# Cross-attention slot sums split between TensorE and VectorE in a decoder layer, with the tick offsets around it moved

## The reference

```python
x = x + attn(layernorm(x))                       # causal, 16 heads of 16
x = x + xattn(ctx, ctx, layernorm(x), ssm, D, 8)  # long convolution of key-value products
x = x + ffn(layernorm(x))                        # 4-bit weights, 256 -> 2048 (gate, up) -> 256
```

```python
kv = einsum('bhil,bhjl->bijhl', k, v)
out = causal_conv(kv, ssm_kernel) + kv * D
out = einsum('bijhl,bhil->bjhl', out, q)
```

## Time and profile before

| | |
|---|---|
| median of 3 runs | 279.81 us |
| the profiled execution | 280.03 us |
| its span, first to last instruction | 278.3 us |
| busy: TensorE (PE) | 250.9 us, 90% |
| busy: VectorE (DVE) | 162.5 us, 58% |
| busy: GpSimd (POOL) | 149.3 us, 54% |
| busy: ScalarE (ACT) | 129.9 us, 47% |
| mean granted TensorE clock | 0.972 of full speed |

### The profile page before, as it was taken

How to read it: one execution, slowest core, us unless ns; L and a number is a source line. 1 busy time by engine, 2 the same in 40 slices (tenths; PEclk the granted TensorE clock), 3 DMA queues, 4 the chain that set the end, 5 groups by cost and what they waited for, 6 DMA issues and landing times.

```text
span 278.3 us, 5004 instructions
## 1 busy us (share of the span) xinstructions
PE 250.9 (90%) x1872; PEld 161.9 (58%) x1872; DVE 162.5 (58%) x280; ACT 129.9 (47%) x281; POOL 149.3 (54%) x172
## 2 busy tenths in 40 slices
PE   7999999965999887895598998999999999999993
PEld 7765775533665655673454655556665566556662
DVE  2888523989786999668658364251725446131114
ACT  2454665545466666764555254331435243432230
POOL 3278464413116596759988995228354554723330
PEclk9999999999799999978979999999999999999998
DMA  6998969130300000000420030000303000000004
GB/s 200 389 318 199 181 224 173 30 114 4 117 1 4 2 1 6 1 2 0 124 102 2 0 115 0 1 4 0 113 2 113 3 2 0 0 2 0 0 2 151
DMA packets 15104, 18.81 MB, mean 68 GB/s; under 512 B 1448, under 2 KB 12776, under 8 KB 15080
## 3 DMA queue, kind: packets, MB, share of 16 engines
q1 hardware_dynamic: 13832, 16.13, 21.4%
q10 hardware_dynamic: 1248, 2.36, 2.7%
HBM read 15.21 MB, written 3.15 MB: 66 GB/s over the span
## 4 chain that ended last, share of the span: by engine, by line
PE 56%; DVE 5%; POOL 4%; issue 3%; ACT 2%; DVEq 0%; POOLq 0%; ACTq 0%
PE bank L980 30%; PE bank L1150 15%; PE bank L1165 2%; PE bank L1163 2%; POOL w L492 1%; PE bank L1177 1%; DVE o_sb L851 1%; POOL arena L476 1%; PE bank L1179 1%; PE bank L1108 1%; DVE XN L946 1%; ACT XN L651 1%; POOL rstd L403 1%; POOL arena L479 1%; PE bank L1203 1%
## 5 line engine op out<-in xcount | busy, mean ns | idle before, releaser
L500 POOL TENSOR_TENSOR QK<-QK 128x512 f16<-128x512 f32 x31 | 35.9, 1160 | 56.0 <-ACT QK L625 56.0
L894 DVE SCALAR_TENSOR_TENSOR QK<-bank,QK 128x512 f32<-128x512 f32 x32 | 22.0, 689 | 61.2 <-PE bank L980 61.2
L635 ACT ACTIVATE QK<-bank 128x512 f32<-128x512 f32 x32 | 19.1, 597 | 70.5 <-PE bank L980 70.3
L980 PE MATMUL bank<-xTh,Wa 128*128 128x512 f16 x128 | 41.9, 389 | 0.0
L980 PE MATMUL bank<-xTh,Wb 128*128 128x512 f16 x128 | 40.7, 379 | 0.0
L476 POOL TENSOR_TENSOR arena<-Ys,qx 128x640 f32<-128x640 f32 x16 | 25.1, 1568 | 2.0 <-ACT qx L665 2.0
L980 PE MATMUL bank<-xTl,Wa 128*128 128x512 f16 x64 | 25.0, 391 | 0.0
L980 PE MATMUL bank<-xTl,Wb 128*128 128x512 f16 x64 | 24.3, 379 | 0.0
L816 DVE TENSOR_REDUCE mx<-bank 128x8 f32<-128x1024 f32 x16 | 19.4, 1212 | 7.7 <-PE bank L1073 7.6
L1150 PE MATMUL bank<-Wa,QK 128*128 128x256 f16 x192 | 23.6, 273 | 0.0
L403 POOL TENSOR_TENSOR rstd<-veps,nhalf 128x1 f32<-128x1 f32 x16 | 9.6, 597 | 25.6 <-ACT veps L643 25.6
(11 more groups left out here) (145 smaller groups left out, 509.8 us busy)
## 6 DMA issues: line engine op xcount, KB each, us to landing
arena<-in_ker SPq DMA_DIRECT2D x2, 1024.0 KB, 12.0
QK<-qk_scratch SPq DMA_DIRECT2D x8, 256.0 KB, 5.9
arena<-in_ctx SPq DMA_DIRECT2D x2, 768.0 KB, 7.8
qk_scratch<-Wa SPq DMA_DIRECT2D x12, 128.0 KB, 3.4
arena<-in_codes SPq DMA_DIRECT2D x4, 384.0 KB
QK<-qk_scratch SPq DMA_DIRECT2D x8, 128.0 KB, 5.8
arena<-in_gu_scale SPq DMA_DIRECT2D x4, 256.0 KB
out<-XN SPq DMA_DIRECT2D x4, 256.0 KB, 2.4
```

The lines of the kernel that those rows point to most:

```text
L500: g_.tensor_tensor(il[:, u % IR], val[:, u % VR], ih[:, u % IR], ALU.subtract).then_inc(s_il, 1)
L635: s_.activation(val[:, u % VR], bank[2 * (u % 2)][:, :], ACT.Gelu_apprx_tanh, scale=1.0 / W_GAIN).then_inc(s_gel, 1)
L894: v_.scalar_tensor_tensor(out=val[:, u % VR], in0=bank[2 * (u % 2) + 1][:, :], scalar=UP_SCALE, in1=val[:, u % VR], op0=ALU.mult, op1=ALU. ...
L980: ins = mmul(out, a(c), w(c), start=(n == 0), stop=(n == 3 * len(chunks) - 1))
```

## The change

- The half 1 of the slot sums leaves VectorE. In `T_RT` TensorE adds it from Z directly: eight float32 matmuls, one for each slot, whose stationary operand is every eighth word of Z's second half. R keeps half 0 and becomes half as large. The step waits for the reduce only after the residual's matmul, and then for the second half of Z.
- `T_MIX2` goes from 12 to 11, `T_SPLIT` from 1 to 2, `T_PROJ` from 9 to 8 (and behind `T_ATT` in its tick, which leaves its place in the cyclic order as it was). `CONV_RATE` goes from 2 to 1. Units 6 and 7 and the decoding of groups 2 and 3 come one tick earlier. TICKS stays 30.
- The order of steps within a tick is another on every engine. On TensorE the query's transposes (`T_QT`) go ahead of the scores, and `T_YT` ahead of the transposed scores.

```diff
-        R = sb("R", [P, 2, 2 * H, HD])
+        R = sb("R", [P, 2, H, HD])
...
-         T_QT, T_MIX, T_MIX2, T_SUM, T_SUM2, T_RT, T_LN3, T_RSTD3, T_APPLY3, T_YT) = (
-            0, 1, 3, 4, 5, 6, 7, 7, 8, 9, 8, 9, 9, 10, 11, 12, 12, 12, 13, 13, 14, 15, 15)
+         T_QT, T_MIX, T_MIX2, T_SUM, T_RT, T_LN3, T_RSTD3, T_APPLY3, T_YT) = (
+            0, 2, 3, 4, 5, 6, 7, 7, 8, 8, 8, 9, 9, 10, 11, 11, 12, 13, 13, 14, 15, 15)
-        CONV_RATE = 2
+        CONV_RATE = 1
-        UNIT_TICKS = (22, 23, 24, 24, 25, 26, 28, 29)
+        UNIT_TICKS = (22, 23, 24, 24, 25, 26, 27, 28)
-        DECODE = (1, 5, 19, 23)
+        DECODE = (1, 5, 18, 22)
...
                 if lc == 0:
                     pool.wait_ge(s_qx, 2 * b + 2)
                     if b >= 2:
-                        pool.wait_ge(s_r, 2 * (b - 1))
+                        pool.wait_ge(s_r, b - 1)
+                elif b >= 2:
+                    pool.wait_ge(s_rt, b - 1)
...
-            def sum_slots(b, half):
+            def sum_slots(b):
-                ve.wait_ge(s_z, 4 * b + 2 * half + 2)
+                ve.wait_ge(s_z, 4 * b + 2)
-                v_.tensor_reduce(R[:, b % 2, H * half:H * half + H],
-                                 view(Z[:, b % 2], [[NSLOT, H * HD], [1, NSLOT]], 1024 * half),
+                v_.tensor_reduce(R[:, b % 2], view(Z[:, b % 2], [[NSLOT, H * HD], [1, NSLOT]]),
                                  AX.X, ALU.add).then_inc(s_r, 1)
...
                     take(6, s_x2, b + 1)
-                    pe.wait_ge(s_r, 2 * b + 2)
                     pe.wait_ge(s_x1, b + 1)
                     mmul(bank[6][:, 0:D], ident[:, :], X[:, b, :], start=True, stop=False, skip_group_check=True)
-                    for c in range(2):
-                        last = mmul(bank[6][:, P * c:P * c + P],
-                                    R[:, b % 2, H * c:H * c + H, :].rearrange("p h i -> p (h i)"),
-                                    ident[:, :], start=False, stop=(c == 1), skip_group_check=True)
+                    pe.wait_ge(s_r, b + 1)
+                    mmul(bank[6][:, 0:P], R[:, b % 2].rearrange("p h i -> p (h i)"),
+                         ident[:, :], start=False, stop=True, skip_group_check=True)
+                    pe.wait_ge(s_z, 4 * b + 4)
+                    for slot in range(NSLOT):
+                        last = mmul(bank[6][:, P:2 * P], view(Z[:, b % 2], [[NSLOT, P]], 1024 + slot),
+                                    ident[:, :], start=False, stop=(slot == NSLOT - 1), skip_group_check=True)
                     last.then_inc(s_rt, 1)
```

More of the change, by code:

```diff
@@ L504, in _ @@
             for t in range(TICKS):
-                for b in batch(t, T_MIX2):
-                    conv_products(b, 1)
+                for j in early_decode(t, 2):
+                    decode_scale(j, 1)
+                for b in batch(t, T_MIX):
+                    conv_products(b, 0)
                 for b in batch(t, T_RSTD3):
@@ L509, in _ @@
                     rstds(2, b, 1)
-                for j in early_decode(t, 2):
-                    decode_scale(j, 1)
+                for b in batch(t, T_RSTD2):
+                    pool.wait_ge(s_veps[1], b + 1)
+                    rstds(1, b, 1)
+                for b in batch(t, T_MIX2):
+                    conv_products(b, 1)
+                for j in early_decode(t, 1):
+                    decode_scale(j, 0)
                 for h in conv_heads(t + 1):
@@ L514, in _ @@
                         products(h)
[L515 to L521, removed]
                 for u in early_units(t):
@@ L657, in _ @@
             for t in range(TICKS):
+                for b in batch(t, T_LN3):
+                    sc.wait_ge(s_rt, b + 1)
+                    s_.activation(X[:, b, :], bank[6][:, 0:D], ACT.Copy).then_inc(s_x2, 1)
+                for b in batch(t, T_RSTD3):
+                    ln_eps(2, b)
+                for b in batch(t, T_APPLY3):
+                    ln_apply(2, b)
+                for b in batch(t, T_MPT):
+                    sc.wait_ge(s_mpt, b + 1)
+                    if b >= 2:
+                        sc.wait_ge(s_rows[b % 2], 32 * (b // 2))
+                    s_.activation(mT[:, b % 2, :], bank[7][0:2 * H, 0:P],
+                                  ACT.Copy).then_inc(s_mt, 1)
+                    exp_max(b)
+                for h in conv_heads(t):
+                    conv_out(h, 0)
+                    conv_out(h, 1)
+                for b in batch(t, T_OT):
+                    sc.wait_ge(s_ot, b + 1)
+                    if b >= 2:
+                        sc.wait_ge(s_proj, b - 1)
+                    s_.activation(oT[:, b % 2], bank[7][:, 0:D].rearrange("p (c t) -> p c t", c=2),
+                                  ACT.Copy).then_inc(s_ott, 1)
                 for b in batch(t, T_QT):
@@ L667, in _ @@
                                   ACT.Copy).then_inc(s_qx, 1)
[L668 to L687, removed]
                 for b, p in pair_of_groups(t, T_ST):
@@ L691, in _ @@
                     pv_out(b)
+                for b in batch(t, T_LN2):
+                    sc.wait_ge(s_proj, b + 1)
+                    s_.activation(X[:, b, :], bank[7][:, 0:D], ACT.Copy).then_inc(s_x1, 1)
                 for b in batch(t, T_RSTD2):
                     ln_eps(1, b)
+                for b in batch(t, T_APPLY2):
+                    ln_apply(1, b)
                 for u in early_units(t):
                     unit(u)
+                for j in early_decode(t, 2):
+                    w_hi_step(j)
+                    if j + 1 < EARLY:
+                        load_codes(sc, j + 1)
                 for b in batch(t, T_YT):
@@ L700, in _ @@
                                   ACT.Copy).then_inc(s_yth, 1)
[L701 to L712, removed]
             for u in range(2 * EARLY, UNITS):
@@ L879, in w_lo @@
                                         op0=ALU.mult, op1=ALU.subtract).then_inc(s_ffl, 1)
-            def sum_slots(b, half):
-                ve.wait_ge(s_z, 4 * b + 2 * half + 2)
-                if half == 0 and b >= 2:
+            def sum_slots(b):
+                ve.wait_ge(s_z, 4 * b + 2)
+                if b >= 2:
                     ve.wait_ge(s_rt, b - 1)
-                v_.tensor_reduce(R[:, b % 2, H * half:H * half + H],
-                                 view(Z[:, b % 2], [[NSLOT, H * HD], [1, NSLOT]], 1024 * half),
+                v_.tensor_reduce(R[:, b % 2], view(Z[:, b % 2], [[NSLOT, H * HD], [1, NSLOT]]),
                                  AX.X, ALU.add).then_inc(s_r, 1)
@@ L897, in _ @@
             for t in range(TICKS):
[L898 to L905, removed]
                 for h in conv_heads(t + 1):
@@ L908, in _ @@
                         products(h)
+                for b in batch(t, T_SUM):
+                    sum_slots(b)
+                for b, p in pair_of_groups(t, T_SCORES):
+                    pair_max(b, p)
+                for j in early_decode(t, 3):
+                    w_lo(j)
+                for b in batch(t, T_LN3):
+                    ve.wait_ge(s_x2, b + 1)
+                    ln_stats(2, b)
+                for b in batch(t, T_SPLIT):
+                    max_pieces(b)
                 for b in batch(t, T_LN2):
@@ L915, in _ @@
                     codes_join(j)
[L916 to L920, removed]
                 for b in batch(t, T_NORM):
@@ L1157, in _ @@
             for t in range(TICKS):
[L1158 to L1163, removed]
+                for b in batch(t, T_QT):
+                    take(6, s_qx, 2 * b + 2)
+                    pe.wait_ge(s_xn[1], b + 1)
                     for c in range(2):
-                        last = mmul(bank[7][:, 0:D], oT[:, b % 2, c, :], wo[:, c, :], start=False, stop=(c == 1))
-                    last.then_inc(s_proj, 1)
+                        last = t_.transpose(bank[6][:, P * c:P * c + P], XN[:, b, P * c:P * c + P], ident[:, :])
+                    last.then_inc(s_qt, 1)
                 for b, p in pair_of_groups(t, T_SCORES):
@@ L1186, in _ @@
                     mmul(bank[7][0:2 * H, 0:P], mp[:, b % 2, :], identh[:, :], start=True, stop=True).then_inc(s_mpt, 1)
[L1187 to L1197, removed]
+                for h in conv_heads(t):
+                    convolve(h, 0)
+                    convolve(h, 1)
                 for b in batch(t, T_YT):
@@ L1204, in _ @@
                     last.then_inc(s_yt, 1)
+                for b, p in pair_of_groups(t, T_ST):
+                    if p == 0:
+                        pe.wait_ge(s_rows[b % 2], 32 * (b // 2 + 1))
+                    scores_t(b, p)
                 for b in batch(t, T_TOK):
@@ L1223, in _ @@
                     attend(b, g)
+                for b in batch(t, T_PROJ):
+                    take(7, s_x1, b + 1)
+                    pe.wait_ge(s_ott, b + 1)
+                    if b == 0:
+                        pe.wait_ge(s_w[3], 16)
+                    mmul(bank[7][:, 0:D], ident[:, :], X[:, b, :], start=True, stop=False)
```

(6 more changed lines are left out.)

## The result

The changed kernel takes 317.64 us (median of 4 runs, 313.87 to 320.99) against 280.26 us: a ratio of 1.1305, 95% interval 1.1239 to 1.137. It is 37 us slower, and the forecast was 286.9. The sign was right; the size lies far outside the range of 277 to 296.

What follows compares the result with a forecast made beforehand. PE's order was taken to bound most periods, GpSimd one. Convolutions -4.3, QT +1.7, periods +5.3 and late ticks +4.4 sum to +7.1 us on 280.03, 287.1, or 286.9 us as median; range 277 to 296.

Steps and rivals of the forecast that it cites:

- What bounds it: From the first RT, PE's order from T_OT to the suffix sum plus some 3 us of normalising, not the busy DVE.
- the four periods that PE sets: Periods from 91.15 to 129.33 us: RT's added passes count whole, less 0.6 us of reduce wait, +5.7 us.
- the one that GpSimd sets: Period from 129.33 to 138.74 us: GpSimd bounds it, so b4's added passes hide in PE's idle time, 0 us.
- the late ticks: 138.74 to 177.50 us: +4.7 for three RTs, -1.6 for idle time that goes, +1.3 before unit 8, sum +4.4 us.
- The added passes: Eight matmuls in RT in place of one, strided loads hidden behind the passes: net +1.58 us a batch.
- the upper bound of 3.06: RT's added passes if every strided load stands in full between passes: 3.06 us a batch.
- The rival to which I gave 0.17: Strided loads stall in RT, 3.06 instead of 1.58 us a batch: 297.3 us, partly hidden, some 296; chance 0.17.
- QT: QT ahead of both scores on PE: they wait behind it for ScalarE's layernorm, +1.7 us, +1.1 in the first such tick.
- The convolutions: One head a tick takes 5.7 us of PE work from before the first row maxima: -4.3 us, bounds 0 and -6.4.
- The wait before unit 8: Unit 8 right behind the last YT waits for ScalarE's and DVE's parts, unit 7 no longer between: +1.3 us.
- Idle time: Added passes run where PE waits for normalise in five periods: -3.4 us in all, 276.4 us; chance 0.23.
- The clock did not stay up: Rival: busier PE keeps 2.4 GHz in stretches that ran at 1.2 GHz, -4.9 us, 282.0 us; chance 0.10.

Runs made afterwards that it cites:

- e4: Kernel before with the slot sums split onto TensorE, old ticks and orders, GpSimd writing Z's second half so operands are adjacent words: 288.13 us, ratio 1.0293.
- e6: e2 with TensorE's YT put back behind the transposed scores: 288.9 us, ratio 1.0249 to the kernel before.
- e7: e6 with QT also put back, behind both scores and ahead of OT: 288.19 us, ratio 1.0245 to the kernel before.
- e13: e7 with old unit and decoding ticks, PROJ at the head of the next tick and max_pieces at offset 1: 281.51 us, ratio 1.0055.
- e14: e13 with GpSimd's old ticks and order put back: 281.34 us, ratio 1.0021 to the kernel before.
- e16: Kernel before with one convolution head a tick and, on VectorE, max_pieces ahead of the decoding of its tick: 276.18 us, ratio 0.9829.
- e17: e16 plus the wait of e12: 273.57 us, ratio 0.9731 to the kernel before.
- e2: The change's moved ticks, rates and orders alone, with VectorE still summing both halves: 291.68 us, ratio 1.0451 to the kernel before.
- e1: Kernel before with the split slot sums alone, every eighth word, on the old ticks and orders: 303.79 us, ratio 1.085.
- e5: Changed kernel with steps of 8, 1, 2, 4, 3, 6, 5, 7 words in RT's stationary operand for batches 0 to 7; one run, 312.09 us, wrong sums.
- e12: Kernel before, with GpSimd starting Z's second half only after o_sb of two batches later, for batches 0 to 2: 279.7 us, ratio 0.9974.

## Why the prediction was wrong

**What bounds it: right.** DVE looked full and was not the bound. e4 takes 9.3 us of work from it and is 8.4 us slower, 2.1 less than the sum of its own steps. Stage by stage, where passes keep their pace: the four periods that PE sets grow by 4.8 us (5.7 by the prediction), the one that GpSimd sets by 0.1 (0), the late ticks by 2.3 (4.7), and the first `T_OT` comes 1.2 later (0), in single profiles.

**The added passes: the first step that failed.** "I take 1.58, since YT's row shows a longer load, and I know of no stall behind it." A batch paid 16 x 0.239 - 0.225 = 3.6 us, over even the upper bound of 3.06, since a step of eight words costs more than YT's step of two on which both bounds stood. YT's row could not tell: step 2 is the last that costs next to nothing, 2.06 us for sixteen passes against 1.95. The rival to which I gave 0.17 had the mechanism that happened, and it decided 15.7 us, though its own price of 297.3 was far too low. The rule of the Trainium skill (SBUF — State Buffer, Door 1: The DMA port swizzle) had spoken for it.

**YT was never priced.** The prediction counted QT's new place and passed over YT's: its list of what is queued behind RT has YT ahead of ST, but it puts no price on that. It passed over ScalarE's new order too, in which YT's operand stands behind the copy that waits for RT. e6 puts 5.6 us on YT's place on TensorE, of the orders' 12.0.

**QT: +1.7, not resolved.** The first period did grow by 1.1, from 7.1 to 8.2 us, as worked out. But e7 against e6 shows no change in the time.

**The convolutions: "I take -4.3".** In the changed kernel the first `T_OT` came at 76.5, not 71.5. The mechanism exists: with `max_pieces` ahead of the decoding it comes at 69.5 to 72.3 (e13, e14, e16, e17). The change itself had moved `max_pieces` a tick later, behind the decoding of tick 1. I had counted that move as a possible gain of up to 0.4. PE then sat idle 1.21 and 2.46 us and more of the stretch ran at 1.2 GHz: its granted clock is 0.90, against 0.95 before. The clock is not what kept the gain away: in e2, with the same orders, it is 0.95 there, and the first `T_OT` still comes at 76.2.

**The late ticks: +4.4, measured +14.6.** In e2, without the passes, the stretch takes 42.4 us, so 3.6 are the moved orders and 11.0 the passes, near 3 x 3.6 = 10.8. On the old orders the same passes cost 6.9 there (e1, 45.6 us), with a granted clock of 1.00 against 0.96. The wait before unit 8 was worked out at 1.3; from YT's start at 213.69 us to unit 8 is 1.34 us, 0.94 of it idle:

```profile
213.69 0.40 PE L1194 MATMUL bank<-ident,XN 128*128 128x128 f32 x2
215.03 0.39 PE L979 MATMUL bank<-xTh,Wa 128*128 128x512 f16 x1 [0.94 <-DVE xTl L924]
```

**The other rivals.** Idle time did not take the passes, with a strided load or without: e4 still pays 8.4 of 10.5. The clock did not stay up: 0.957 over the whole, against 0.972.

**What stays open.** 1.3 us of the 37.4 are not in the three parts. Of the orders' 12.0, runs of their own show YT's place on TensorE (5.6) and that of `max_pieces` (5.4). The second is an earlier start than the kernel before has: e13 and e14 reach the old time by it, and pay for something else in the periods and the late ticks. What QT, the tail's ticks, PROJ and GpSimd's order cost one by one is below what their runs tell, and ScalarE's and VectorE's orders were never put back alone.

## What to carry to other kernels

Before work moves onto TensorE from a strided buffer, lay the buffer out so that each stationary operand is adjacent; here GpSimd could write it either way at the same price. When a step moves within an in-order engine, ask for every shared bank who must have read it, what its operand's producer now waits for first, and what used to run meanwhile. And a gain upstream is only worth what the next producer lets through: one head a tick gave nothing until the maxima went ahead of the decoding, and then the two gave 1.7%.

## What was not expected of the hardware

- Passes of float32 with 128 columns cost 0.122, 0.129, 0.185 and 0.244 us at steps of 1, 2, 3 and 4 words of the stationary operand (the lengths of e5's lines over 16, which are some 0.01 over the spacing), and 0.23 to 0.24 beyond.
- Some operations of VectorE that start while GpSimd multiplies (L476 or L492) end 0.03 to 0.3 us after GpSimd's, and others are not held up. o_sb took 1.72 us in the kernel before against 0.42 once GpSimd waits (e12), and the small operations of `max_pieces` up to 1.66 against 0.18 to 0.23. Beside the same L476, the reciprocal just ahead of o_sb kept its 0.25 us, num, which reads a bank, its 0.44, and the reduces of slot sums their 1.2.
